# One exponential a unit, rounded by VectorE; the diagonal of the maxima made by GpSimd

## The reference

```
x = layernorm(x + attention(x, x, causal))          # self
x = layernorm(x + attention(x, context))            # cross
x = layernorm(x + moe(x))    # 8 experts, 2 picked a token, hidden size 512
attention: softmax(q k^T / sqrt(8)) v, per batch row (64 queries, 64 keys) and head
```

## Time and profile before

| | |
|---|---|
| median of 3 runs | 798.61 us (795.01 to 799.62) |
| profiled execution | 803.89 us, span 802.1 us |
| busy share of the span | PE 74%, VectorE 61%, ScalarE 57%, GpSimd 46% |
| mean granted TensorE clock | 0.876 |
| VectorE's waits before the row maxima | 78.6 us, for the scores (L1501) |
| TensorE's waits before `turn_o` | 71.6 us, for the outputs `o_n` (L1108) |

### The profile page before, as it was taken

The page is one execution under the profiler, slowest core; times in us unless marked ns, Lnnn a source line. Parts: engine busy times, 40 slices in busy tenths (PEclk is TensorE's granted clock), DMA queues, the critical chain, the costliest instruction groups (busy, mean ns, idle before and its releaser), DMA issues. The chain is left out here.

```text
span 802.1 us, 21265 instructions
## 1 busy us (share of the span) xinstructions
PE 596.7 (74%) x7870; PEld 471.7 (59%) x7870; DVE 488.9 (61%) x1337; ACT 453.3 (57%) x824; POOL 370.1 (46%) x576
## 2 busy tenths in 40 slices
PE   2776676776767698887987988698777776878970
PEld 1344444545444476765766776476666666777870
DVE  3465879767696877888776578866334651221153
ACT  1223545444333589977997889688467554334320
POOL 7122243433337544435753665387237476530350
PEclk9965878877757999998999999899989888899995
DMA  4351554843132645544655675546546457778730
GB/s 111 106 174 54 161 170 128 287 125 87 34 93 66 198 146 168 164 130 139 195 155 177 185 205 171 151 140 174 162 142 191 141 176 222 234 239 266 234 96 20
DMA packets 141413, 124.64 MB, mean 155 GB/s; under 512 B 12224, under 2 KB 123600, under 8 KB 141312
## 3 DMA queue, kind: packets, MB, share of 16 engines
q1 hardware_dynamic: 134496, 113.06, 46.6%
q0 software_dynamic: 4368, 9.05, 4.1%
q10 hardware_dynamic: 2448, 1.18, 0.5%
HBM read 86.81 MB, written 38.54 MB: 156 GB/s over the span
## 5 line engine op out<-in xcount | busy, mean ns | idle before, releaser
L1089 DVE TENSOR_REDUCE row_max<-bank 128x16 bf16<-128x1024 f32 x64 | 78.3, 1224 | 79.4 <-PE bank L1501 78.6
L776 POOL TENSOR_TENSOR prob_lo<-probT,prob_hi 128x384 f16<-128x384 f32 x64 | 68.7, 1073 | 92.8 <-ACT prob_hi L892 92.4
L1549 PE MATMUL bank<-consts,o_n 128*128 128x64 f32 x256 | 47.7, 316 | 81.2 <-DVE o_n L1108 71.6
L1628 PE MATMUL bank<-w_in,w_hl 128*128 128x128 f32 x704 | 106.3, 298 | 0.0
L1549 PEld LDWEIGHTS bank<-consts,o_n 128*128 128x128 f32 x256 | 39.3, 220 | 95.3 <-issue 71.0
L1628 PEld LDWEIGHTS bank<-w_in,w_hl 128*128 128x128 f32 x704 | 93.8, 207 | 0.4
L889 ACT ACTIVATE probT<-bank 128x1024 f32<-128x1024 f32 x64 | 65.6, 1024 | 46.2 <-PE bank L1525 45.8
L762 POOL TENSOR_TENSOR veps<-mv,eps 128x1 f32<-128x1 f32 x64 | 14.5, 226 | 140.3 <-DVE mv L1127 140.3
L799 POOL DMA_INDIRECT w_hl<-ys,pos x60 | 59.6, 994 | 40.5 <-DMA ys<-w_hl 23.5
L1614 PE MATMUL bank<-xT,w_in 128*128 128x128 f16 x1056 | 77.9, 226 | 0.0
L1082 DVE TENSOR_TENSOR prob_lo<-probT,prob_hi 128x640 f16<-128x640 f32 x64 | 62.3, 973 | 24.9 <-ACT prob_hi L892 24.8
(11 more groups left out here) (173 smaller groups left out, 1556.8 us busy)
## 6 DMA issues: line engine op xcount, KB each, us to landing
w_in<-w_scr SPq DMA_DIRECT2D x96, 512.0 KB, 3.7
q_scr<-q_hl SPq DMA_DIRECT2D x64, 128.0 KB
k_scr<-k_hl SPq DMA_DIRECT2D x64, 128.0 KB, 2.3
q_st<-q_scr SPq DMA_DIRECT2D x32, 256.0 KB, 3.9
k_all<-k_scr SPq DMA_DIRECT2D x128, 64.0 KB, 2.1
xs_tile<-xs SPq DMA_DIRECT2D x42, 128.0 KB
ys<-w_hl SPq DMA_DIRECT2D x42, 128.0 KB, 2.1
xs<-xs_tile SPq DMA_DIRECT2D x3, 1472.0 KB, 6.8
```

The lines of the kernel that those rows point to most:

```text
L776: pool.tensor_tensor(p_lo[u.buf][:, h, :], probT[u.buf][:, h, :], p_hi[u.buf][:, h, :], ALU.subtract).then_inc(lo_second[u.kind], 1)
L1089: dve.reduce_max(row_max[u.buf][:, :], bank[:, SC:SC + 2, :].rearrange("p a (h k) -> p (a h) k", k=S), AX.X).then_inc(max_done[a], 1)
L1549: last = pe.matmul(turned_o[:, 64 * b:64 * b + 64], o_n[u.buf][:, b, :, :, :].rearrange("p c a d -> p (c a d)"), consts[:, C_DELTA:C_TRI], ...
L1628: last = pe.matmul(expert_y(x), hid[x.par][:, c, :], w2_t[x.wb][:, c, :], start=False, stop=c == FC - 1, skip_group_check=True)
```

## The change

- ScalarE computes the exponential once, to f32 `probT`, and signals.
- VectorE makes `p_hi` from it by a copy f32 to f16 of all 1024 columns, waits for that copy, and subtracts all 16 heads (1024 columns) to `p_lo`. GpSimd has no part in it any more.
- VectorE's `maxima` ends with the reduction. GpSimd makes `max_diag`, in `spread_maxima`, which stands in its slot behind `gain` and ahead of the scatters and gathers.
- `weigh` waits for one semaphore in place of two.

```diff
@@ gpsimd
-            def probs_low(u):
-                pool.wait_ge(exp_done[u.kind], u.count())
-                h = slice(DVE_HEADS, H)
-                pool.tensor_tensor(p_lo[u.buf][:, h, :], probT[u.buf][:, h, :], p_hi[u.buf][:, h, :], ALU.subtract).then_inc(
-                    lo_second[u.kind], 1)
+            def spread_maxima(u):
+                pool.wait_ge(max_done[u.kind], u.count())
+                m = row_max[u.buf][:, :].rearrange("p (a c) -> p a c", c=2).unsqueeze(2).to_broadcast([P, HP, S, 2])
+                dl = neg_delta.rearrange("p (q c) -> p q c", c=2).unsqueeze(1).to_broadcast([P, HP, S, 2])
+                pool.tensor_tensor(max_diag[u.buf][:, :, :, :], dl, m, ALU.mult).then_inc(diag_ready[u.kind], 1)
...
                 if u := unit_at(g - 4):
                     gain(u)
+                if u := unit_at(g):
+                    spread_maxima(u)
                 for c, n, k in scatters_at(g):
                     scatter(c, n, k)
...
-                if u := unit_at(g - 1):
-                    probs_low(u)
                 if u := unit_at(g - 3):
                     spread(u)
@@ scalar, exps
                 act.activation(probT[u.buf][:, :, :].rearrange("p h q -> p (h q)"),
-                               bank[:, KEYS:KEYS + 2, :].rearrange("p a n -> p (a n)"), ACT.Exp,
-                               scale=float(HD) ** -0.5)
-                act.activation(p_hi[u.buf][:, :, :].rearrange("p h q -> p (h q)"),
                                bank[:, KEYS:KEYS + 2, :].rearrange("p a n -> p (a n)"), ACT.Exp,
                                scale=float(HD) ** -0.5).then_inc(exp_done[a], 1)
@@ vector
-            def probs_low(u):
+            def probs_low(u, v):
                 dve.wait_ge(exp_done[u.kind], u.count())
-                h = slice(0, DVE_HEADS)
-                dve.tensor_tensor(p_lo[u.buf][:, h, :], probT[u.buf][:, h, :], p_hi[u.buf][:, h, :], ALU.subtract).then_inc(
-                    lo_first[u.kind], 1)
+                if v:
+                    dve.wait_ge(pv_ready[v.kind], v.count())
+                dve.tensor_copy(p_hi[u.buf][:, :, :], probT[u.buf][:, :, :]).then_inc(hi_done[u.kind], 1)
+                dve.wait_ge(hi_done[u.kind], u.count())
+                dve.tensor_tensor(p_lo[u.buf][:, :, :], probT[u.buf][:, :, :], p_hi[u.buf][:, :, :], ALU.subtract).then_inc(
+                    lo_done[u.kind], 1)
@@ vector, maxima
-                dve.wait_ge(max_done[a], u.count())
-                m = ...
-                dl = ...
-                dve.tensor_tensor(max_diag[u.buf][:, :, :, :], dl, m, ALU.mult).then_inc(diag_ready[a], 1)
@@ tensor, weigh
-                pe.wait_ge(lo_first[a], u.count())
-                pe.wait_ge(lo_second[a], u.count())
+                pe.wait_ge(lo_done[a], u.count())
```

More of the change, by code:

```diff
@@ L25 @@
 CLEAR_SLOT, CLEAR_EVERY = 10, 2
-DVE_HEADS = 10
 CHUNK = (3, 4, 4, 4, 1)
@@ L491, in build @@
         v_hi_ready = two("v_hi_ready")
-        lo_first, lo_second = two("probs_lo_first_heads"), two("probs_lo_second_heads")
+        hi_done, lo_done = two("probs_hi"), two("probs_lo")
         lg_ready, lg_done, route = sem("lg_ready"), sem("lg_done"), sem("route_step")
@@ L1090, in maxima @@
                                bank[:, SC:SC + 2, :].rearrange("p a (h k) -> p (a h) k", k=S), AX.X).then_inc(max_done[a], 1)
-                dve.wait_ge(max_done[a], u.count())
-                m = row_max[u.buf][:, :].rearrange("p (a c) -> p a c", c=2).unsqueeze(2).to_broadcast([P, HP, S, 2])
-                dl = neg_delta.rearrange("p (q c) -> p q c", c=2).unsqueeze(1).to_broadcast([P, HP, S, 2])
-                dve.tensor_tensor(max_diag[u.buf][:, :, :, :], dl, m, ALU.mult).then_inc(diag_ready[a], 1)
             def outputs(u):
@@ L1359, in slot @@
                 if u := unit_at(g - 1):
-                    probs_low(u)
+                    probs_low(u, same_buffers(g - 1))
                 if u := unit_at(g - 2):
```

## The result

The changed kernel takes 908.4 us (906.3 to 910.3, 4 runs) against 799.0 us (795.0 to 799.6, 4 runs): a ratio of 1.138, 95% interval 1.1335 to 1.1425. The forecast was 905 us, range 840 to 955. The profiled execution took 910.25 us, span 908.5 us, with a mean granted clock of 0.825.

What follows compares the result with a forecast made beforehand. Bound: the in-order ring of VectorE and TensorE. Collision 104 us less 17 under waits is 87, plus 5 at the ends and 15 for the clock: 107 on 803.9, 911 profiled; median 905 us, range 840 to 955.

Steps and rivals of the forecast that it cites:

- The ring of VectorE and TensorE: Reduction through outputs to TensorE's line 1549, 4.61 us, then scores for the next reduction; sets the slot, tight in 33.
- The order: copy, GpSimd's multiply, subtraction: After the reduction GpSimd's multiply runs between VectorE's two instructions: 3.80 us against 1.81, +1.97 us a slot, 104 us.
- Prices: Lengths of the three added instructions: rounding copy 0.69 us, full subtraction 1.24 with start-up, GpSimd's multiply 2.15.
- Cover in the 20 late slots: Second-stage slots where TensorE was said to wait for ScalarE's expert-tile copy: 17 us of added time hidden.
- The ends: Eleven units before 86.5 and after 548.9 us, paced by transfers and expert tiles: 5 us together.
- The clock: TensorE idles more and clocks lower: 0.5 us a first-stage slot, 0.15 a second-stage slot, 15 us (0 to 40).
- GpSimd's queue: Multiply placed ahead of scatters and rstd; said to be over before rstd's statistics come, so no cost counted.
- The rival without collision: Between copy and subtraction the multiply does not hold VectorE up: +0.1 us a slot, 793 to 805 us; chance 12%.
- the rival in which scatters get in as well: One to three scatters behind the multiply also delay VectorE's subtraction: 25 to 76 us more, about 955; chance 12%.
- ScalarE's second exponential: Its removal, 1.02 us a unit, counted as 0: off the ring in 33 slots, only shortening a wait in 20.

Runs made afterwards that it cites:

- e5: Kernel before, with VectorE's subtraction of the low parts moved behind the outputs and the residual: 777.5 us, ratio 0.974.
- e6: Changed kernel, with VectorE's copy and subtraction moved behind outputs and residual: 790.5 us, ratio 0.988 against the kernel before.
- e12: Kernel before, with VectorE's subtraction moved behind outputs and residual and its diagonal behind the outputs: 772.1 us, ratio 0.966.
- e2: Changed kernel, but VectorE makes the diagonal again, so GpSimd has neither diagonal nor subtraction: 834.5 us, ratio 1.048 against the kernel before.
- e3: Changed kernel, with GpSimd's multiply made to wait until VectorE has subtracted the previous unit: 855.4 us, ratio 1.076 against the kernel before.
- e11: Changed kernel, with GpSimd's multiply split into two instructions of 512 columns each: 875.9 us, ratio 1.098 against the kernel before.
- e10: Changed kernel, with GpSimd's scatters moved behind rstd: 897.5 us, ratio 1.125 against the kernel before.
- e8: Changed kernel, with 8 unread matmuls of 512 columns added at the end of TensorE's slots 10 to 31: 900.0 us, ratio 1.126.
- e1: Kernel before, with only the diagonal moved from VectorE to GpSimd, both exponentials and the split subtraction kept: 822.0 us, ratio 1.033.
- e4: Changed kernel, with GpSimd's multiply done twice, first to a spare tile: 955.7 us, ratio 1.201 against the kernel before.

## Why the prediction was right, point by point

- **The ring of VectorE and TensorE.** Right. `turn_o` starts 0.15 us behind the outputs in the mean of the first stage, before and after. e5, e6 and e12 change nothing but the order of VectorE's work in it and take 19.5, 118 and 27 us off the kernel that each starts from (the last from the kernel before).
- **The order: copy, GpSimd's multiply, subtraction.** Right in 50 of 53 slots, and shown four ways: by the slot above, by its absence when the diagonal is taken back (e2) or made to wait (e3), and by the half dose (e11, 4.90 us as written down). The slots of e10 in which the multiply comes late say the same. That GpSimd waits for the copy too, for which the prediction had no row, the slot above shows.
- **Prices.** Copy 0.69 us forecast, 0.688 measured. Subtraction 1.24 and 1.23. The multiply was put at 2.15 us and takes 1.89: that is the term that was mis-sized. From 384 columns in 0.92 us to 1024 in 1.89 it is 1.5 ns a column, where the rows with fewer columns had given 1.8 to 2.1. From the reduction to the outputs a slot grew by 1.54 us (82 us in the 53 slots), not by 1.97 (104). Of the 22 us between, 14 are the multiply's length and 4 the three slots without a contest; the last 4 are not taken apart, probably starts that overlap. From the reduction to `turn_o` 6.5 us were forecast, and it is 5.9.
- **Cover in the 20 late slots.** Forecast 17 us, measured 13. The reason given was wrong in the main: TensorE was late there because it was still at its own matmuls. In 7 of the 20 it did not wait at all, and in the others its idle time ahead of line 1549 was mostly 0.37 to 0.39 us, 6 us in all of the 21.6. The ends: forecast 5, measured 5.
- **The clock.** Forecast 15 us. "Back" grew by 32 us. In the first stage its 9 us are the clock's: e8 gives them back. In the second, 23 us, the clock over the "back" parts fell from 0.94 to 0.74; how much of the 23 is the clock's was not measured by itself. The forecast counted nothing for GpSimd's queue, since the multiply would be over before rstd is wanted. The multiply is over (3.6 us after the reduction's start, rstd begins at 7.0), but the scatters behind it push rstd to 8.4. That costs little here: "back" grew by 0.78 us in the 12 slots with scatters and by 0.62 in the 22 without, which leaves some 2 us for the queue, by an estimate. The 11 us of e10 are mostly contests that no longer take place.
- So the profiled execution comes out at 910.3 us for 911 by luck: 22 us too much for the part from reduction to outputs, 17 too little for what lies behind `turn_o`, and 4 too much taken off for cover. The median missed by 3.4 us, since the changed kernel's lies only 1.8 us under its profiled execution and 5.3 were assumed.
- **The rival without collision** is refuted by the subtraction's 2.80 us, **the rival in which scatters get in as well** by its maximum of 2.803 us: VectorE's subtraction never waited for more than one instruction. The trace before already spoke against that rival: of 13 subtractions that ran beside a scatter 12 took 0.81 to 0.85 us, and only the one of the earlier trace rows took 1.96.
- **ScalarE's second exponential** was counted at 0 on this ring. No run takes it out alone, so that is not shown by itself; e2, which takes it out and gives VectorE the copy, is 35 us slower. ScalarE's busy time fell by 53 us (453.3 to 399.9) and not by the 65 us of its instructions, since their spans overlap their neighbours'; VectorE's grew by 98 us where I had said over 100.

## What to carry to other kernels

Find the ring of waits that sets the slot before counting busy shares: ScalarE was 81% busy in a stage of the kernel before, and at the same order of VectorE's work the kernel without its second exponential is slower than the one with it (908 against 799 us, 790 against 778), since VectorE and GpSimd got other work for it. Look for pairs of VectorE and GpSimd instructions on SBUF that start at one event: here the price of the moved instruction was its whole length on the other engine, and it was paid because VectorE, which had to wait for it, is on the ring. In e1, where mostly GpSimd had to wait, the first stage even got shorter. First take off the ring what nobody wants yet (here two moves of a few lines, 3.4%); then check what the moved instruction meets next, as e6's rstd did.

## What the runs showed of the hardware

- VectorE's copy or two-input subtraction and GpSimd's multiply or subtraction hold each other up for nearly the whole instruction: 2.80 us for 1.23, 2.27 for 1.89.
- Who waits takes its turn between two instructions of the other, in both directions: GpSimd between VectorE's copy and subtraction, VectorE between GpSimd's two multiplies (e4) and between its two halves (e11). The earlier trace rows is an exception that no run here explains: there VectorE's subtraction began 0.34 us ahead of GpSimd's, behind a scatter, and ended 0.69 us after it.
- A GpSimd instruction of a single column can wait for a full VectorE subtraction: 1.54 us for 0.54 (e6).
- GpSimd's multiply of 1024 bf16 columns takes 1.89 us. That is 1.5 ns for each column beyond the 384 that take 0.92 us in f32 and f16, less than between the smaller instructions of the earlier trace rows.
